# A cross-attention kernel on one core: the running maximum one tile later, four of six tile pairs summed in plain float32, and one subtraction per half moved from VectorE to GpSimd

## The reference

```python
q = (hidden @ Wq).reshape(B, Sq, H, D);  k = (ctx @ Wk).reshape(B, Skv, H, D);  v = (ctx @ Wv)...
q = rmsnorm(q, gq); k = rmsnorm(k, gk)            # mean square over D=128, per key and head
scores = einsum("bqhd,bkhd->bhqk", q, k) / sqrt(D)
attn = softmax(scores)                            # over 1500 keys
out = einsum("bhqk,bkhd->bqhd", attn, v) ... @ Wo
x = layernorm(x + out)
```

## Time and profile before

| | us |
|---|---|
| median of 3 runs (1316.31 to 1316.51) | 1316.31 |
| profiled execution | 1316.16 |
| its span | 1314.4 |
| one phase in the steady stretch | 65.71 |
| busy: TensorE, VectorE, ScalarE, GpSimd | 1242.9, 1170.7, 971.3, 1061.6 |

### The profile page before, as it was taken

One profiled execution on the slowest core, in us unless ns is written; L12 is line 12 of the kernel. 1 busy time (PEld: TensorE's weight loads), 2 busy tenths in 40 slices (PEclk: granted clock), 3 DMA queues, 4 the chain that ended last, 5 costly groups with the idle time before them and its releaser, 6 DMA issues.

```text
span 1314.4 us, 24031 instructions
## 1 busy us (share of the span) xinstructions
PE 1242.9 (95%) x6024; PEld 958.7 (73%) x6024; DVE 1170.7 (89%) x4434; ACT 971.3 (74%) x4019; POOL 1061.6 (81%) x937
## 2 busy tenths in 40 slices
PE   8889989999999999999999999999999999999998
PEld 5767656677777777777777777777777777778787
DVE  5865679999999999999999999999999999997655
ACT  2667886888888888888888888888888888863342
POOL 5744452889898989898989898989898989997740
PEclk9999999999999999999999999999999999999999
DMA  7050240101010101010101010101010101030300
GB/s 255 34 197 1 73 168 18 54 25 48 24 48 25 48 25 48 24 48 24 48 24 48 24 48 24 48 25 48 24 48 25 48 24 48 1 112 1 135 4 28
DMA packets 34106, 66.55 MB, mean 51 GB/s; under 512 B 3056, under 2 KB 22640, under 8 KB 32176
## 3 DMA queue, kind: packets, MB, share of 16 engines
q1 hardware_dynamic: 32976, 64.66, 14.8%
q10 hardware_dynamic: 992, 0.36, 0.1%
HBM read 56.89 MB, written 8.13 MB: 49 GB/s over the span
## 4 chain that ended last, share of the span: by engine, by line
POOL 45%; PE 31%; issue 15%; DVE 6%; ACT 2%; DMA 1%; POOLq 0%; ACTq 0%; DVEq 0%
POOL xa_den L1225 18%; POOL probs_r L1239 8%; POOL xa_scores L1214 6%; PE om_ps L1586 3%; PE xa_o_ps L1579 3%; POOL xa_ctx_m L1175 2%; POOL xa_den L1232 2%; POOL xa_q_lo L1149 2%; POOL xa_nat_r L1245 2%; PE xq_ps L636 2%; POOL ctxT_lo L1155 2%; PE xa_k_ps L1496 1%; DVE xa_k_ps L1393 1%; PE xa_k_ps L1485 1%; PE xa_s_ps L1485 1%
## 5 line engine op out<-in xcount | busy, mean ns | idle before, releaser
L1323 ACT ACTIVATE xa_k_ps<-xa_k_ps 125x128 f32<-125x128 f32 x1536 | 399.3, 260 | 61.9 <-PE xa_k_ps L1487 59.7
L1393 DVE CUSTOM_DVE_ANT_0 xa_k_ps<-xa_k_ps,xa_ctx_m 125x128 f32<-125x128 f32 x1536 | 399.1, 323 | 16.7 <-PE xa_k_ps L1497 14.5
L1323 ACT ACTIVATION_READ_ACCUMULATOR xa_k_ps<-xa_k_ps 125x1 f32 x1536 | 283.7, 185 | 0.0
L1225 POOL TENSOR_TENSOR xa_den<-probs,xa_den 125x896 f32<-125x896 f32 x128 | 271.6, 2122 | 5.8 <-ACT probs L1306 5.8
L1408 DVE TENSOR_TENSOR xa_scores<-xa_s_ps,xa_rk 125x448 f32<-125x448 f32 x384 | 238.1, 620 | 11.1 <-PE xa_s_ps L1487 11.0
L1496 PE MATMUL xa_k_ps<-wk_parts,xa_ctxT_hi 128*125 128x512 f32 x384 | 208.1, 542 | 34.3 <-ACT xa_k_ps L1323 30.0
L1306 ACT ACTIVATE probs<-xa_scores 125x896 f32<-125x896 f32 x192 | 181.7, 946 | 71.4 <-issue 45.7
L1393 DVE DVE_READ_ACCUMULATOR2_ANT xa_ss<- 125x1 f32 x1536 | 218.7, 142 | 0.0
L1422 DVE TENSOR_TENSOR xa_max_ps<-xa_scores,xa_max_ps 125x448 f32<-125x448 f32 x320 | 200.9, 628 | 9.9
L1239 POOL TENSOR_TENSOR probs_r<-probs,xa_p_hi 125x896 fp32r<-125x896 f32 (+1 forms) x96 | 197.7, 2059 | 0.6
L1579 PE MATMUL xa_o_ps<-probs,xa_ctx_nat 125*128 125x448 f32 x396 | 181.5, 539 | 0.0
(11 more groups left out here) (193 smaller groups left out, 2615.2 us busy)
## 6 DMA issues: line engine op xcount, KB each, us to landing
xa_ctx_m<-in_ctx SPq DMA_DIRECT2D x48, 250.0 KB
xa_ctx_nat<-in_ctx SPq DMA_DIRECT2D x16, 750.0 KB
ctxT_in<-in_ctxT SPq DMA_DIRECT2D x84, 125.0 KB, 2.1
qo<-in_xo_w SPq DMA_DIRECT2D x1, 2048.0 KB, 15.8
qo<-in_xq_w SPq DMA_DIRECT2D x1, 2048.0 KB, 16.1
vo_scratch<-qo SPq DMA_DIRECT2D x2, 1024.0 KB, 4.0
w_parts_scratch<-ws_hi SPq DMA_DIRECT2D x2, 1024.0 KB, 6.2
w_parts_scratch<-ws_lo SPq DMA_DIRECT2D x2, 1024.0 KB, 7.2
```

The source lines that it names most:

```text
L1225: pool.tensor_tensor(den2[:, :, :], probs_pair(y), so_far, ALU.add).then_inc(den_done, 1)
L1323: last = act.activation(cols, cols, ACT.Square, scale=MEAN ** 0.5, accum_out=ss[:, j // 2, head:head + 1])
L1393: form = dve.tensor_tensor_reduce(cols, cols, ctx_m[:, j // 2, :], 2 * MEAN, 0.0, ALU.mult, ALU.add, ss[:, j // 2, head:head + 1])
```

## The change

VectorE's step takes the maximum one tile later (the last tile's at the start of the next half, ahead of the forms); VectorE shifts three pairs in a half in place of four, at t = 2, 4 and 6; GpSimd shifts three in place of two (pair 6 at t = 8 is new); pair 6 is no longer split, so that L1308, L1239 and the three products of its tiles fall away and a plain product comes in; the natural-order context is rounded in two parts in place of three, at j = 19 and 21 on ScalarE and j = 20 and 23 on GpSimd (before: two parts at j = 17 and 18, one at 21 and 23). In the last phase each split pair has one split tile, as before.

```diff
-VECTOR_SHIFTS = {2: 0, 3: 2, 5: 4, 7: 6}
-VS, GS = 4, 2
+VECTOR_SHIFTS = {2: 0, 4: 2, 6: 4}
+VS, GS = 3, 3
...
-FIRST_SPLIT = 3
-PAIR_SPLITS = (0, 0, 0, 2, 2, 2)
+FIRST_SPLIT = 4
+PAIR_SPLITS = (0, 0, 0, 0, 2, 2)
-LAST_SPLITS = (0, 0, 0, 1, 1, 1)
-NAT_PARTS = slice(6, 8), slice(8, 10), slice(10, 12)
-LAST_PARTS = slice(7, 8), slice(9, 10), slice(11, 12)
-NAT_ENDS = 8, 10, KT
+LAST_SPLITS = (0, 0, 0, 0, 1, 1)
+NAT_PARTS = slice(8, 10), slice(10, 12)
+LAST_PARTS = slice(9, 10), slice(11, 12)
+NAT_ENDS = 10, KT
...
-NAT_HI_AT = {17: (0, 1), 21: (2,)}
-NAT_LO_AT = {18: (0, 1), 23: (2,)}
+NAT_HI_AT = {19: (0,), 21: (1,)}
+NAT_LO_AT = {20: (0,), 23: (1,)}
...
+            def running_max(ph, j):
+
+                h, t = divmod(j, KT)
+                dve.wait_ge(s_taken, pos_s(ph, j) + 1)
+                wait(dve, max_done, ph.at(2 * (KT - 1), (KT - 1) * h + t - 1))
+                if t == KT - 1:
+                    wait(dve, max_turned, ph.at(2, h))
+                dve.tensor_tensor(cmax[0:KP, :] if t == KT - 1 else max_ps[0:KP, 0:UW], score_slot(ph, j),
+                                  max_ps[0:KP, 0:UW], ALU.max).then_inc(max_done, 1)
+
             def body(ph):
                 for j in range(STEPS):
                     h, t = divmod(j, KT)
...
+                    if t == 0 and ended_half(ph, h):
+                        running_max(ph if h else ph.shift(-1), (j - 1) % STEPS)
                     if ph.within(-1, 14):
...
+                        take_forms(ph, j)
                     if ph.within(0, 15):
...
                         dve.tensor_tensor(scores[0:KP, ph.at(STEPS, j) % SC, :, :], raw, key_scale, ALU.mult
                                           ).then_inc(s_taken, 1)
 
+                    if ph.within(0, 15) and t >= 2:
+                        running_max(ph, j - 1)
                     if t == MAX_TURN and ended_half(ph, h):
...
-                    if ph.within(0, 15) and t >= 1:
-                        dve.wait_ge(s_taken, pos_s(ph, j) + 1)
-                        wait(dve, max_done, ph.at(2 * (KT - 1), (KT - 1) * h + t - 1))
-                        if t == KT - 1:
-                            wait(dve, max_turned, ph.at(2, h))
-                        dve.tensor_tensor(cmax[0:KP, :] if t == KT - 1 else max_ps[0:KP, 0:UW], score_slot(ph, j),
-                                          max_ps[0:KP, 0:UW], ALU.max).then_inc(max_done, 1)
```

More of the change, by code:

```diff
@@ L1378, in _, with take_forms @@
             link = linker(dve, mlp.dve_chain)
+            def take_forms(ph, j):
+                if j % (2 * MT) == 0:
+                    dve.wait_ge(m_ready, m_count(ph, j // (2 * MT)))
+                dve.wait_ge(k_done, ph.at(2 * STEPS, 2 * STEPS + 2 * j + 1))
+                for g in range(GH):
+                    cols = k_ps[0:KP, (2 * j) % 3, g * C:(g + 1) * C]
+                    head = UH * (j % 2) + g
+                    form = dve.tensor_tensor_reduce(cols, cols, ctx_m[:, j // 2, :], 2 * MEAN, 0.0, ALU.mult, ALU.add,
+                                                    ss[:, j // 2, head:head + 1])
+                form.then_inc(formed, 1)
+            def running_max(ph, j):
[6 more added lines that the diff above has]
+                                  max_ps[0:KP, 0:UW], ALU.max).then_inc(max_done, 1)
             def body(ph):
```

## The result

The changed kernel takes 1324.85 us (median of 4 runs, 1324.43 to 1325.62) against 1316.31 for the kernel before in the same rounds: a ratio of 1.0066, 95% interval 1.0048 to 1.0083. It is slower, by 8.5 us or 0.7%; the interval does not reach 1. Its profiled execution took 1324.81 with a span of 1322.8.

What follows compares the result with a forecast made beforehand. It took VectorE to bound the first half and GpSimd the second, then a handshake loop through GpSimd's L1199. Terms +10.5, -1.5 and +0.9 made +9.9 on 1316.16, so 1326 us, range 1300 to 1336 (own range 1319 to 1333).

Steps and rivals of the forecast that it cites:

- The two small terms: Phase 0, bound by VectorE, saves 1.5 us; phases 15 and 16, bound by TensorE, lose 0.9 to six plain tiles.
- the main term: Phases 1 to 14 each 0.75 us longer through the loop over GpSimd, +10.5 us.
- VectorE's step: Later maximum starts 0.54 us behind L1408, not 0.65; a step without a shift goes from 2.15 to 2.03.
- Point 1: From GpSimd's L1155: pair 10's exponential 2.87 us, then VectorE's first shift 3.88 later, at 6.75, both unchanged.
- Points 2 and 3: VectorE's third shift ends 11.2 us after its first starts; ScalarE then lets L1199 start at 20.65, second half 21.0.
- Point 4: GpSimd by itself reaches L1199 at 20.55 us (first half, 1.5 idle before L1163) and 19.2 (second, then waits 1.8).
- Points 5 and 6: L1199 to half's end takes 11.4 and 13.4 us; halves 32.05 and 34.4, phase 66.45 against 65.71.
- Other signs: In the changed trace: VectorE idle 1 to 2 us before its first shifts; TensorE's wait at j = 19 gone.
- GpSimd is not held: Rival, 23%: L1199 never waits for ScalarE, GpSimd's own list sets 64.6 us a phase; 1300 us, faster.
- The later maximum saves nothing: Rival, 9%: VectorE's new operand order gains nothing, phase 0.92 us longer, +13 and no phase 0 gain; 1341 us.
- TensorE became the bound: Rival, 5%: TensorE's list of 62.2 us a phase sets the time; 1267 us.
- The two halves balance: Rival, 10%: ScalarE's path to L1199 is 0.3 to 0.5 us shorter each half, phase within 0.2 of 65.71; 1316 us.

Runs made afterwards that it cites:

- either repair or both: Changed kernel with VectorE's shifts at t = 2, 3, 5: 1308.76 us; with natural part at j = 20 and 22: 1311.61; with the two together: 1297.43.
- the last experiment: Changed kernel with four shifts on VectorE (t = 2, 3, 5, 7) and natural part at j = 20 and 22: 1269.21 us, ratio 0.9643 to the kernel before.
- the maximum alone: Kernel before with only VectorE's maximum taken one tile later, splits and shifts as before: 1304.64 us against 1316.31.

## Why the prediction was right

- **Sum.** Forecast +9.9 on 1316.16, measured 1324.81 - 1316.16 = +8.65 for the two profiled executions. A phase became 0.67 longer in place of 0.75; over the 13.5 phases from 250.01 to 1136.40 in the trace before, from 249.95 to 1145.07 after, that is +8.73, where 10.5 was forecast for fourteen. The two small terms were wrong: phase 0 saved 0.06 and not 1.5, as step 20 began 1.67 earlier (237.71 against 239.38) and not 3.5, and then lost 1.6 to the new shift and natural part; the end, from those marks on, gave -0.3 and not +0.9 (177.7 against 178.0 us). That -0.3 is a sum of opposite pieces, as TensorE's score products show: the delay of 8.7 falls to 6.2 early in phase 15 and grows back to 8.4. The plain products are in it at the size forecast: two tiles of phase 15 are 2.66 and 2.65 apart (1212.20, 1214.86, 1217.51) where they were 2.53 and 2.51 (1204.11, 1206.64, 1209.15). The errors of the two small terms, +1.4 and -1.2, nearly cancelled, which was luck; the -1.8 of the main term remains, against a miss of 1.3 in all.
- **VectorE's step.** 0.53 from L1424 to L1399 and 2.02 a step (821.90 to 823.92) against 0.54 and 2.03 forecast. The experiment without it shows the value in the whole: 17.6 us. The Trainium skill ("VectorE: DVE Perf Modes", "The DRAIN you can't avoid") reports eight chained copies that took the same time with and without semaphores between them. That a wait is free doesn't carry over to this kernel: both orders have the same operations and the same number of them wait, and the order in which the result waited for is already old is faster by 0.12 us an operation.
- **Point 1.** 813.18 to 816.05 is 2.87, and 816.05 to 819.94 is 3.89: as forecast.
- **Points 2 and 3.** 819.94 to the end of the third shift, 831.10, is 11.16 (11.2 forecast). L1199 started at 20.95 of the second half (21.0) and 20.63 of the first (20.65).
- **Point 4.** GpSimd was at L1199 by itself at 19.33 of the second half (20.95 less its 1.62 idle; 19.2 forecast), and idle 1.49 at L1163 of the first (1.5).
- **Points 5 and 6.** 11.45 and 13.35 behind L1199 (11.4 and 13.4); halves of 32.08 and 34.30 (32.05 and 34.4).
- **Other signs.** VectorE stood 1.25 and 1.13 us in front of its first shifts (1 to 2 forecast), and TensorE's wait of 1.70 us at j = 19 (at 694.75 before) is gone.
- **The rivals.** "GpSimd is not held" falls on the 1.62 at L1199; when the hold was made shorter, by either repair or both, the time fell to 1297 to 1312, around the 1300 of that rival, though L1199 of the second half still waited for L1328 in all three. "The later maximum saves nothing" was put at 1341; with the maximum undone the kernel takes 1342.44. TensorE became the bound only in the last experiment; the phase of 62.2 put down for it came out at 62.41 there. "The two halves balance" falls on the halves: 32.08 and 34.30.
- **Where my working was off.** The claim that only VectorE's third shift holds L1328 was too narrow: behind it stands ScalarE's queue at j = 19, at 19.9 to 20.5 by itself. In the change, where L1199 starts at 20.95, it was hidden by some 0.5 to 1 us; it showed when the shift was taken forward. And VectorE's list before is 32.14 a half, not the some 32.3 behind my 30.3: the 32.64 of the first half came from the path through VectorE to the denominator, not from its list alone.

Where the 8.5 us come from can be read in steps, each a kernel of the table. Later maximum and plain pair together give 1316.31 - 1279.89 = -36.4. Moving the shift of pair 6 to GpSimd, with the others left at t = 2, 3 and 5, gives 1308.76 - 1279.89 = +28.9, about the 30.2 that it costs in the kernel before. Spreading the other two to t = 4 and 6 gives 1324.85 - 1308.76 = +16.1. So the moved shift ate most of the gain, and it is the spreading, which moves no work between engines, that made the change slower than the kernel before: without it the change would have been 7.5 us faster. My prediction had the step of delay in its point 2, but did not say that the sign hangs on it.

## What to carry to other kernels

When three engines are 94 to 97% busy, the shares do not say whose work is dear: write the loop of handshakes from one instruction to its next instance, with start-to-start distances, and see for every moved instruction on which side of a wait it lands. An instruction taken from the busiest engine can lengthen the loop twice: by its time on the other engine (28.9 us here), and by the steps that its neighbours shift when the order is spread out again (16.1). And of two orders with the same work, measure both: two shifts one step earlier and one natural part later turned 1325 us into 1297 with every instruction on the engine where it was, and with the moved shift back on VectorE into 1269.

## What the runs showed of the hardware that I had not expected

A VectorE operation that reads its predecessor's result, and waits for it, starts 0.65 us behind it, one that reads an older result 0.53 to 0.54, for 448 columns of float32. The prediction took that from two distances; its size over a kernel, 12 us (the maximum alone) to 18 us (inside the change), is what the runs add. Whether the reading or the waiting costs the 0.12 is not shown, as every such operation here does both.
